# The first edge loads of a four-layer graph kernel move from SP's queue to ACT's

## The reference

```python
# x (32, 256, 128) float32, adj (32, 256, 256) int32
h = relu(layernorm(x)); x = x + gat(h, adj, W0, a0)            # layer 0
h = relu(layernorm(x)); x = x + multi(h, adj, a0, a1, a2, a3)  # layer 1
h = relu(layernorm(x)); x = x + rgcn(h, adj, weight, bias)     # layer 2
h = relu(layernorm(x)); x = x + elu(gat(h, adj, W3, a3))       # layer 3

def gat(h, adj, W, a):
    Wh = h @ W
    e = leaky_relu((Wh @ a[:128])[:, :, None] + (Wh @ a[128:])[:, None, :], 0.2)
    return softmax(where(adj > 0, e, -9e15)) @ Wh
def multi(h, adj, ...):   # score of the pair by its relation r = 1..4
    e_r = leaky_relu((h * a_r) @ h.T, 0.2); picked where adj == r, else -9e15
    return softmax(e) @ h
def rgcn(h, adj, weight, bias):
    return sum_r((adj == r) @ h @ weight[r]) + bias
```

## Time and profile before

| | us |
|---|---|
| median of 3 runs | 291.73 |
| lowest, highest | 291.55, 292.25 |
| the profiled execution | 291.89 |
| its span, first to last instruction | 290.1 |
| busy in the span: PE, ACT, DVE, POOL | 275.5, 259.7, 251.4, 235.6 |

### The profile page before, as it was taken

The page is one execution under the profiler, slowest core; times in us unless marked ns, Lnnn a source line. Parts: engine busy times, 40 slices in busy tenths (PEclk is TensorE's granted clock), DMA queues, the critical chain, the costliest instruction groups (busy, mean ns, idle before and its releaser), DMA issues.

```text
span 290.1 us, 8093 instructions
## 1 busy us (share of the span) xinstructions
PE 275.5 (95%) x2250; PEld 257.0 (89%) x2250; DVE 251.4 (87%) x1217; ACT 259.7 (90%) x850; POOL 235.6 (81%) x376
## 2 busy tenths in 40 slices
PE   2899999999999999999998999999999999999992
PEld 1799998898899999999978899988899999999991
DVE  4788999988888888999988899988878988799985
ACT  4799998999997888898999899899999788889984
POOL 4799876886658999999999988786765799999922
PEclk9999999999999999999999999999999999999998
DMA  5935555500000000011111470000000000001123
GB/s 183 340 105 164 166 166 163 163 5 0 2 1 2 0 2 3 2 54 58 54 49 47 163 239 2 3 0 2 1 2 1 1 2 0 2 5 55 57 71 113
DMA packets 15949, 17.77 MB, mean 61 GB/s; under 512 B 2720, under 2 KB 11808, under 8 KB 15904
## 3 DMA queue, kind: packets, MB, share of 16 engines
q1 hardware_dynamic: 15488, 17.18, 18.6%
q10 hardware_dynamic: 416, 0.07, 0.1%
HBM read 13.05 MB, written 4.19 MB: 59 GB/s over the span
## 4 chain that ended last, share of the span: by engine, by line
PE 63%; POOL 10%; DVE 9%; ACT 8%; issue 7%; DMA 1%; SPq 0%; DVEq 0%; POOLq 0%; ACTq 0%
PE bank L987 20%; PE bank L934 10%; PE bank L929 6%; PE bank L905 5%; PE bank L863 5%; PE bank L954 5%; POOL h L365 3%; DVE pT L688 3%; PE bank L984 3%; PE bank L972 3%; POOL rs L356 3%; PE bank L942 2%; PE bank L936 2%; POOL h L373 2%; ACT relu_y L556 2%
## 5 line engine op out<-in xcount | busy, mean ns | idle before, releaser
L356 POOL TENSOR_TENSOR rs<-mv,minus_half 128x2 f32<-128x2 f32 x128 | 91.5, 715 | 37.8 <-DVE mv L624 36.3
L987 PE MATMUL bank<-val,pT 128*128 128x129 f32 x512 | 74.6, 275 | 0.0
L987 PEld LDWEIGHTS bank<-val,pT 128*128 128x128 f32 x512 | 67.8, 193 | 0.0
L688 DVE SCALAR_TENSOR_TENSOR pT<-bank,val,edgesT 128x256 f32<-128x256 f32 x128 | 55.6, 476 | 5.9 <-ACT edgesT L503 3.1
L373 POOL TENSOR_TENSOR h<-h,rs 128x256 f32<-128x256 f32 x93 | 57.8, 621 | 1.8
L613 DVE BATCH_NORM_STATS2 st<-x 128x6 f32<-128x128 f32 x192 | 45.6, 279 | 0.0
L905 PE MATMUL bank<-w_gat,hT 128*128 128x131 f32 x256 | 41.0, 284 | 2.8 <-ACT hT L484 2.8
L516 ACT ACTIVATE val<-bank,val 128x128 f32<-128x128 f32 x128 | 41.8, 397 | 0.1
L365 POOL TENSOR_TENSOR h<-x,mv 128x256 f32<-128x256 f32 x64 | 41.3, 645 | 0.2
L863 PE MATMUL bank<-ident,h 128*128 128x128 f32 x192 | 38.0, 280 | 1.0 <-POOL h L373 0.7
L905 PEld LDWEIGHTS bank<-w_gat,hT 128*128 128x128 f32 x256 | 34.4, 194 | 4.8 <-ACT val L516 3.5
(11 more groups left out here) (85 smaller groups left out, 651.5 us busy)
## 6 DMA issues: line engine op xcount, KB each, us to landing
edges<-in_adj SPq DMA_DIRECT2D x32, 256.0 KB, 3.3
xin<-in_x SPq DMA_DIRECT2D x32, 128.0 KB, 2.4
out_x<-result SPq DMA_DIRECT2D x32, 128.0 KB, 1.7
w_rel<-in_L_gnn_weight SPq DMA_DIRECT2D x1, 256.0 KB, 3.2
w_gat<-in_L_gnn_W ACTq DMA_DIRECT2D x1, 64.0 KB, 2.7
w_gat<-in_L_gnn_W SPq DMA_DIRECT2D x1, 64.0 KB, 3.2
a_rel<-in_L_gnn_a SPq DMA_DIRECT2D x4, 0.5 KB, 3.8
bias<-in_L_gnn_bias SPq DMA_DIRECT2D x1, 64.0 KB, 3.4
```

What stands on the lines that cost most here:

```text
L356: pool.tensor_tensor(rs[:, g % WIDE], mv[:, g % WIDE, :, 1], minus_half[:, :], ALU.pow).then_inc(rs_ready, 1)
L688: last = dve.scalar_tensor_tensor(pT[:, n % 4, u], bank_z(n)[:, 0], val[:, k, u, D + 2:D + 3], edgesT[:, g % WIDE, u], ALU.max, ALU.mult)
L987: last = pe.matmul(bank_o(n)[:, t], pT[:, n % 4, u, t * P:(t + 1) * P], values[:, u], start=(u == 0 and layer == 1), stop=(u == T - 1), sk ...
```

## The change

ACT issues the edge loads of graphs 0 to 3, behind its own two loads and ahead of its first calculating instruction. SP no longer issues these; its list becomes x0, x1, x2, x3, x4, edges 4, x5, edges 5, the last layer's weights and vector a, x6, edges 6, x7, edges 7, x8 to x11, and the rest as before. Semaphores, tiles and all later loads are unchanged.

```diff
@@ -24,6 +24,7 @@
 
 
 SLOTS = 8
+ON_ACT = 4
 EARLY = 3
 HS = 12
 XS = 12
@@ -287,9 +288,9 @@
 
             for k in range(XS):
                 sp.dma_start(xin[:, k].rearrange("p t d -> p (t d)"), x_v[k]).then_inc(x_loaded[k], 16)
-                if 1 <= k <= SLOTS:
-                    load_first(k - 1)
-                if k == 2:
+                if ON_ACT <= k < SLOTS:
+                    load_first(k)
+                if k == 5:
                     sp.dma_start(w_gat[1][:, 0:D], w3).then_inc(gat_loaded[1], 16)
                     sp.dma_start(a_gat[1][:, :], a3.rearrange("(c p) o -> p (c o)", c=2), allow_slow_non_contiguous=True).then_inc(gat_loaded[1], 16)
             for r, m in enumerate((m0, m1, m2, m3)):
@@ -434,6 +435,8 @@
 
             act.dma_start(w_gat[0][:, 0:D], w0).then_inc(gat_loaded[0], 16)
             act.dma_start(a_gat[0][:, :], a0.rearrange("(c p) o -> p (c o)", c=2), allow_slow_non_contiguous=True).then_inc(gat_loaded[0], 16)
+            for k in range(ON_ACT):
+                act.dma_start(edges[:, k].rearrange("p t n -> p (t n)"), adj_v[k]).then_inc(edges_loaded[k], 16)
             act.wait_ge(ident_ready, 9)
             act.activation(junk[:, 0:1], ones[:, :], ACT.Exp)
             def scale_a(i):
```

## The result

The changed kernel takes 292.34 us (median of 16 runs, 292.05 to 292.58); the kernel before took 291.73 in 16 runs beside it. The ratio is 1.0016, with a 95% interval of 1.0010 to 1.0023: slower by 0.5 us, between 0.3 and 0.7 (the two medians alone differ by 0.61). The forecast was 292.2, slower by 0.45, called within 0.3% of no change. It is within 0.3%, though sixteen runs do tell it from zero.

What follows compares the result with a forecast made beforehand. Behind the second or third slice the kernel runs at PE's pace, so only a delay of PE's first work counts. Terms +0.45 + 0 + 0 + 0 took the median from 291.73 to 292.2 us, range 291.4 to 293.1.

Steps and rivals of the forecast that it cites:

- Part 1: Head, ACT: four issues ahead of the table load delay the weights' arm and PE's graph 0; +0.45 us (+0.30 to +0.58).
- the list of what was absorbed: Head: of 1.9 us of issues, 0.67 fills ACT's wait for a, 0.2 the copy's gap, 0.35 PE's wait for DVE.
- the 0.35 of slack: PE before graph 0's transposition: the weights' arm was early by 0.35 us (5.68 less 5.33), to absorb part of the delay.
- Part 2: SP's x loads go sooner: DVE's waits before statistics of graphs 2 (0.30) and 3 (0.95) should go; gain 0.
- The slack of 1.15 us: Graph 3: POOL's scaling ends at 11.30, PE transposes at 12.45 without waiting for it, so sooner x gains 0.
- Part 3: Edges share DMA engines with x1 to x4, landing within 5.0 us; masks do not wait; 0 to 0.4, taken as 0.
- Part 4: Last layer's weights go out after x5 at about 4.5 us, needed at 14.82; SP's first list ends 1.9 sooner; 0.
- That the table load might not be held: Rival, ACT's head: the issues do not hold the table load, so the cost is hidden; 291.7 us, chance 0.15.
- The rival of PE's rate: Rival, PE's head: full rate comes one graph later, +0.7 on top of +0.45; 292.9 us, chance 0.13.
- The last step: From the head to the end: all that follows is one chain and takes the 0.45 us along unchanged.

Runs made afterwards that it cites:

- on2: The changed kernel with two edge loads issued on ACT instead of four, the other two back on SP: 291.90 us against 291.67 for the kernel before.
- warm: The kernel before with seven extra transpositions of the identity on PE ahead of its first step: 294.52 us against 291.60.
- split: The changed kernel with its four edge issues on ACT set apart among ACT's first instructions: 291.71 us against 291.67 for the kernel before.
- sp_only: The kernel before with only SP's load order changed (x one place ahead, last layer's weights after x5), no edges on ACT: 291.71 us against 291.60.
- issue_only: The kernel before with four small unread loads issued on ACT ahead of its table load, load lists unchanged: 292.29 us against 291.71.

## Why the prediction was right

**Part 1, four issues ahead of the table load: right in mechanism and size.** Issues ended at 3.60 (said 3.53), table load at 3.63 (3.56), scaling at 5.03 (4.96), copy of the weights at 5.40 (5.35), PE's product at 5.71 (5.68), graph 0 at 6.15 (between 5.98 and 6.26), hT at 6.86 (6.86). The overlap of PE's product with the transposition behind it, which I had left between two bounds, is measured too: the transposition starts 0.44 us into the product's 0.58, halfway between the bounds of 0.30 and 0.58, and so overlaps it by 0.14. The steps fit, but the list of what was absorbed does not add up: 1.9 less 0.67, 0.2 and 0.35 leaves 0.68, not 0.45. The trace has the rest. The delay goes from 1.97 (table load) to 1.20 (scaling), 0.98 (copy), 0.96 (product) and 0.47 (graph 0): 0.77 is absorbed ahead of the scaling, 0.10 of it the pause between the exponential and the scaling beside the idle time named, 0.22 at the copy, and 0.49 at PE, which is the 0.35 of waiting and the 0.14 of overlap. The run with three issues shows the knee where the sum puts it. One term was sharper than the evidence for it: the 0.35 of slack was read off a single execution and moves with the landing of x0 by up to 0.2 us, so that the agreement of 6.86 with 6.86 is in part luck.

**Part 2, x sooner: the value of 0 was right, what DVE would show was half wrong.** The slack of 1.15 us between POOL and PE at graph 3 was real, and the order alone moved nothing (1.0001). But only one of the two waits went, and two new ones came at graphs 5 and 6. The term that was mis-sized is the time of an x load from issue to landing, which I had left as it was. x2 was issued 0.47 sooner (1.65 against 2.12) and took 4.4 us to land where it had taken 3.8, so DVE had it 0.1 later. x6 was issued 0.7 sooner (6.22 against 6.91) and took 5.9 us instead of 4.6, so DVE had it 0.6 later. In the run of the order alone, where SP's queue carries everything, x2 took 3.2 us and both waits are gone. I had also counted SP's issues at 0.476 each to the end. SP in order of time after the change:

```profile
3.54 0.99 SPq L290 DMA_DIRECT2D xin<-in_x  x1
4.57 0.45 SPq L287 DMA_DIRECT2D edges<-in_adj  x1
...
5.56 0.62 SPq L295 DMA_DIRECT2D a_gat<-in_L_gnn_a  x1
6.22 0.47 SPq L290 DMA_DIRECT2D xin<-in_x  x1
```

Up to 3.5 us they keep to it; x5's then takes 0.99 and the vector a's 0.62, so x6 goes out at 6.22, where the count gives 0.74 + 10 x 0.476 = 5.5, and DVE starts on it at 12.18, six microseconds later. With the same order on one queue (the run of the order alone) no issue of the first ten microseconds took over 0.47; that loads from two queues pile up and hold the issues back is my reading of this. It stayed off the path: DVE's combination for graph 0, which stands behind that wait on DVE, is over at 12.58 + 0.86 = 13.44, and PE wants it only at 15.51.

**Part 3, the edges: right.** No mask waited for its edges in the head, and the statistics of graph 1 did not slip (4.07, before 4.04). Landing took 4.5 to 6.5 us instead of 3.9 to 5.0, more than the 5.0 of my bound, and the masks had room for it.

**Part 4, the last layer's weights: right in effect.** They went out at 5.06 instead of the 4.5 I had counted, and PE used them at 15.29. SP's first list ended at 13.33 against 14.09, 0.8 sooner rather than 1.9, because issues grew as in Part 2.

**The rivals.** That the table load might not be held was wrong: it follows the issues in program order in every run (2.18 with one, 3.14 with three, 3.63 with four, 6.12 with eight, 1.66 when they stand behind it). By the Trainium skill, "ScalarE: Activation LUTs", section "What ACT_TABLE_LOAD costs", a drain of some 1.38 us would follow the load. The trace disagrees in the changed kernel too: the exponential starts 1.29 us after the load does. The rival of PE's rate named a real thing and mis-sized it: one more graph at half rate costs 0.2 to 0.5 us (on2, warm) and not 0.7. In the kernel before ACT works without a pause up to its copy of graph 3 at 13.24, so PE is not the only limit there; that this makes the difference was not tested. It fell in neither direction in the profiled execution of the change. By the Trainium skill, "TensorE: Matmul & The Clock Gate", section Part 1, the monitor does not restart with the kernel; that the moment strays between graphs 1 and 2 from run to run agrees. By the Trainium skill's rule in the same section, that activity releases the half rate, one might expect extra work from 2.2 us on to bring the moment forward; in the three traces with such work it did not. The last step, that the head's delay reaches the end unchanged, looks shaken by the profile pair alone (0.2 us between the spans) and holds against the run split (0.46 us late at 15.9, 0.52 at 270.6).

## What to carry to other kernels

A load issued from a calculating engine costs that engine about half a microsecond each, and what matters is what stands behind it in the program: put such issues behind the table load, which they then overlap, rather than ahead of it. That hid four issues, not eight (2.5 us lost), since the next calculating instruction waits for the last issue. Follow the delay along the path and subtract each wait that it fills, until one arm overtakes the other; here 1.9 us came down to 0.45, three issues cost nothing that could be told and the fourth did. Take such a slack from several executions: here it moved by 0.2 us with the landing of one load. An idle time of an engine that waits for a load is no promise of a gain: two of DVE's were removed by the order of the list alone, and the time did not move.

## What the runs showed of the hardware

- ACT's queue issued loads while ACT's calculating part was in its table load: issue at 2.25, load from 2.18 to 3.46. A calculating instruction behind the issues waited for their end: 4.07 behind 4.02, 6.30 behind 6.25.
- An issue took 0.45 to 0.49 us for the first four on ACT and up to 0.83 for one of eight; on SP 0.43 at first and up to 0.99 for one of x. In the head none took over 0.51 where ACT issued no edges (before, sp_only, issue_only); the long ones came where ACT's queue carried edges beside SP's loads. Four loads of 4 KB took as long to issue as four of 256 KB (1.94 us).
- PE's change from half to full rate came at different graphs in different executions, worth up to 0.5 us (0.31 gained in the run of the order alone, 0.47 lost in warm), while the granted clock recorded stayed at 1.00.
- Seven more transpositions in PE's program, at either end of it, lengthened the time behind the last calculating instruction from 2.2 to 5.1 us; eleven lengthened it to 4.8.
- x0 reached DVE between 3.04 and 3.24 us in the nine executions in which it set PE's start, and PE followed 2.44 us later each time.
